# Bias of an FFN sublayer added by a one-row fp32 matmul instead of on VectorE

## The chip, the cores and the metric

The kernel runs on all 8 cores of one Trainium2 chip. Each core takes one batch element (2048 x 1024, fp32) and works alone; the weights are the same for all. The metric is device time in microseconds (us) of the slowest core. Lower is better.

## The reference, cut to what matters

```python
x = x + 0.5 * ffn(layernorm(x), w, bias)
x = x + attn(layernorm(x), Wq, Wk, Wv, W_G, W_O)     # retention, 8 heads, silu gate
x = x + 0.5 * ffn(layernorm(x), w, bias)

def ffn(x, weight, bias):
    # both operands: blocks of 32 along the last axis, scale = max|block| / 7.5,
    # each value / scale rounded to the nearest value of a 6-bit float grid
    xd = quantize(x) * scale_x
    wd = quantize(weight) * scale_w
    return xd @ wd.T + bias
```

The change is about the last line of `ffn`, its bias, and the `x + 0.5 * ...` around it. Both FFN sublayers use the same weight and bias.

## The kernel before, in words

The kernel is written engine by engine, with the order of each engine's work and all semaphore waits set by hand. `emit` is called once for each engine; `c.op(engine, ...)` issues only on that engine and `c.wait(engine, sem, value)` blocks it. Work is in order on each engine. The core's 2048 rows are 16 row chunks `rc` of 128 rows by 1024 columns, and `x_sb` holds all 16 in SBUF.

The program goes: load of x and constants; LayerNorm statistics on ScalarE; quantization and transposition of the FFN weight (first sublayer only, eight chunks); the first FFN's loop over 16 row chunks; the attention sublayer (statistics, transposes, four projections, heads, output projection); LayerNorm statistics; the second FFN's loop; the store.

The loop of `ffn_sublayer`, for row chunk `rc` in program order:

- `q_stageA(rc)` on VectorE: block maxima (TENSOR_REDUCE), scales, reciprocal, scaled values.
- `q_yy(rc)` on ScalarE: squares of these. `x_B2(rc-1)` on VectorE: the end of the previous chunk's rounding, which waits for the previous chunk's cast.
- `ffn_evac(rc-2)` on VectorE: takes the product of chunk `rc-2` out of PSUM. Two instructions: a SCALAR_TENSOR_TENSOR that makes `ffntmp = 0.5 * psum + bias_half`, then a TENSOR_TENSOR `x_sb += ffntmp`. It waits for the matmuls of that chunk (`mm_done[rc-2]`).
- `q_B1(rc)` on VectorE (six instructions), `q_cast(rc)` on ScalarE behind it.
- `x_d(rc+2)` on ScalarE: the activation that centres the rows of a later chunk. Chunks 16 and up do not exist, so the last two rounds have none.
- `x_tr(rc-1)`: eight 128 x 128 transposes on TensorE, each copied out of PSUM by ScalarE, two PSUM tiles in turn. By their semaphore counts the transposes start behind `q_cast(rc)` and `x_d(rc+2)`.
- `x_mm(rc-1)` on TensorE: 16 bf16 matmuls of 128 x 512 into one half of `psc` (two halves of 512 columns, eight contraction chunks each).

So the matmuls that `ffn_evac(rc-2)` waits for were put in motion by the cast at the end of `q_B1(rc-1)`, one round earlier. Behind the loop come `x_B2(15)`, `ffn_evac(14)`, `x_tr(15)`, `x_mm(15)` and `ffn_evac(15)`.

`bias_half` is the bias vector in all 128 partitions. At the start it is multiplied by 0.5 in place on VectorE, behind the wait for the first loads.

In the profile all instructions stand at line 60, that of the helper `op`; they are told apart by engine, operation, tile and shape. `arena` is the SBUF memory, `psc` the PSUM area of the large products, `pt` the two transpose tiles.

Of the kernel before, what the change touches and what calls it, by code (L numbers as in the profile page):

```python
# [12 lines left out]
ALU = mybir.AluOpType  # L13
# [7 lines left out]
KC = 8  # L21
# [62 lines left out]
def build_program(stop_after="full"):  # L84
# [23 lines left out]
    O_C = 196608  # L108
# [12 lines left out]
    def vf32(off, n):  # L121
        return A[:, off:off + 4 * n].bitcast(F32)

    def vbf(off, n):
        return A[:, off:off + 2 * n].bitcast(BF16)
# [4 lines left out]
    x_sb = vf32(O_X, RC * D).rearrange("p (rc d) -> p rc d", d=D)  # L130
# [5 lines left out]
    xdt_sb = vbf(O_V, KC * S).rearrange("p (k n) -> p k n", n=S)  # L136
    g_sb = vbf(O_G, RC * D).rearrange("p (rc d) -> p rc d", d=D)
    wbf_sb = vbf(O_W, KC * D).rearrange("p (k d) -> p k d", d=D)
    wdt_sb = wbf_sb
# [8 lines left out]
    ffntmp = vf32(O_S + 4096, D)  # L148
# [14 lines left out]
    bias_half = vf32(O_C, D)  # L163
# [14 lines left out]
    yv_sb = [vf32(O_C + 9344, 128), vf32(O_C + 9856, 128)]  # L178
    zrow_sb = [vbf(O_C + 10368, 128), vbf(O_C + 10624, 128)]
    negm_sb = vf32(O_C + 10880, 16)  # L180

    sem_ctx = ExitStack()
    sems = {k: sem_ctx.enter_context(nc.semaphore(k)) for k in SEMS}

    def emit(c: Ctx):
# [3 lines left out]
        for i in range(4):  # L189
# [3 lines left out]
             in_=bias_dr.partition_broadcast(128)).inc("ld", 16)  # L193
        c.op("sync", "dma_start", out=m128_sb, in_=m128_dr).inc("ld", 16)
        c.op("sync", "dma_start", out=id_sb, in_=id_dr).inc("ld", 16)
        c.wait("vector", "ld")
        c.op("vector", "tensor_scalar", bias_half, bias_half, 0.5, None,
             ALU.mult).inc("v")
        c.fence()

        def ln_stats(src3d, eps):
# [119 lines left out]
        def ffn_sublayer(build_wdt):  # L321
# [90 lines left out]
            def x_mm(k, s_after):  # L412
                fp = psc[:, (k % 2) * 1024:(k % 2) * 1024 + 1024]
                c.wait("tensor", "s", s_after)
                if k >= 2:
                    c.wait("tensor", "v", ev_done[k - 2])
                for jh in range(2):
                    for kc in range(KC):
                        ins = c.op("tensor", "matmul",
                                   fp[:, jh * 512:(jh + 1) * 512],  # L420
                                   xdt_sb[:, kc, k * 128:(k + 1) * 128],
                                   wdt_sb[:, kc, jh * 512:(jh + 1) * 512],
                                   start=(kc == 0), stop=(kc == KC - 1),
                                   skip_group_check=True)
                        if jh == 1 and kc == KC - 1:
                            ins.inc("t")
                mm_done[k] = c.cnt["t"]

            def ffn_evac(rc):
                fp = psc[:, (rc % 2) * 1024:(rc % 2) * 1024 + 1024]  # L430
                c.wait("vector", "t", mm_done[rc])
                c.wait("vector", "v")
                c.op("vector", "scalar_tensor_tensor", ffntmp, fp, 0.5,
                     bias_half, ALU.mult, ALU.add).inc("v")
                ev_done[rc] = c.cnt["v"]
                c.wait("vector", "v")
                c.op("vector", "tensor_tensor", x_sb[:, rc, :],
                     x_sb[:, rc, :], ffntmp, ALU.add).inc("v")

            x_d(0, max(negm_v, w_end_v))  # L440
            x_d(1, max(negm_v, w_end_v))
            for rc in range(RC):
                if _PARANOID:
                    c.fence()
                c.wait("vector", "s", sd[rc])
                xy[rc] = q_stageA(rc % 2, db[rc % 2], ln_rstd[:, rc:rc + 1])
                xyy[rc] = q_yy(rc % 2, xy[rc])
                if rc >= 1:
                    x_B2(rc - 1)
                if rc >= 2:  # L450
                    ffn_evac(rc - 2)
                xtq[rc] = q_B1(rc % 2, xyy[rc])
                xcast[rc] = q_cast(rc % 2, xtq[rc])
                if rc + 2 < RC:
                    x_d(rc + 2, xxd[rc - 1] if rc >= 1 else xy[rc])
                if rc >= 1:
                    s_after = x_tr(rc - 1)
                    x_mm(rc - 1, s_after)
            x_B2(RC - 1)
            ffn_evac(RC - 2)  # L460
            s_after = x_tr(RC - 1)
            x_mm(RC - 1, s_after)
            ffn_evac(RC - 1)

        ffn_sublayer(build_wdt=True)
# [153 lines left out]
        for hc in range(_NHEADS):  # L619
            for nh in range(2):  # L620
# [20 lines left out]
                for mc in range(MMAX):  # L641
# [10 lines left out]
                    for nb in range(nblo, 2 * nh + 2):  # L652
                        slot = psc[:, (pp % 4) * 512:(pp % 4) * 512 + 512]
                        if piece_rel[pp % 4] is not None:
# [5 lines left out]
                             start=True, stop=True).inc("t")  # L660
# [108 lines left out]
        for rc in range(RC):  # L769
# [10 lines left out]
            for jh in range(2):  # L780
                for kc in range(H):
                    ins = c.op("tensor", "matmul",
                               wp[:, jh * 512:(jh + 1) * 512],
                               zt_sb[:, kc, rc * 128:(rc + 1) * 128],
                               wbf_sb[:, kc, jh * 512:(jh + 1) * 512],
                               start=(kc == 0), stop=(kc == H - 1),
                               skip_group_check=True)
# [23 lines left out]
    with nc.Block() as block:  # L811
        @block.sync
        def _(e):
            emit(Ctx(nc, "sync", sems))

        @block.vector
        def _(e):
            emit(Ctx(nc, "vector", sems))

        @block.scalar  # L820
        def _(e):
            emit(Ctx(nc, "scalar", sems))

        @block.tensor
        def _(e):
            emit(Ctx(nc, "tensor", sems))

        @block.gpsimd
        def _(e):
            emit(Ctx(nc, "gpsimd", sems))  # L830
# [38 lines left out]
```

How the kernel before makes its waits and increments, by code:

```python
    def inc(self, sem, n=1):  # L42
        self.ctx.cnt[sem] += n
        if self.inst is not None:
            self.inst.then_inc(self.ctx.sems[sem], n)
        return self
# [16 lines left out]
    def wait(self, eng, sem, val=None):  # L63
        v = self.cnt[sem] if val is None else val
        if v <= 0:
            return
        if self.cur == eng:
            getattr(self.nc, eng).wait_ge(self.sems[sem], v)
```

## Time and profile before

| | us |
|---|---|
| median of 3 runs | 1866.97 (1866.2 to 1868.91) |
| the profiled execution | 1866.82 |
| its span, slowest core (core 2) | 1865.2 |
| spans of the 8 cores | 1858.7 to 1865.2 |
| VectorE busy | 1053.2 (56%) |
| TensorE matmul busy | 762.2 (41%) |
| ScalarE busy | 535.8 (29%) |

The span is from the first to the last instruction on the core; the execution's own time is 1.6 us more. Busy shares are means over stages that have different limits. The first FFN's loop lies between about 232 and 557 us, the second one's between about 1515 and 1836 us. The granted TensorE clock (PEclk) is a share of 2.4 GHz: 1.00 is 2.4 GHz and 0.50 is 1.2 GHz.

### The profile page before, as it was taken

The numbers are of one execution on the slowest core, as the hardware profiler recorded it, in microseconds if no ns is written. First come the engines' busy times: TensorE is split into PE (matmuls) and PEld (weight loads), VectorE is DVE, ScalarE is ACT, GpSimd is POOL, SyncE is SP. The second block draws the span as 40 slices with busy tenths as digits, with TensorE's granted clock in tenths as the row PEclk, the third lists the DMA queues.
The fourth block names the chain that finished last, engine by engine and source line by source line (L and its number), as shares of the span: only waits on it lengthen the run. The fifth ranks groups of instructions, "written<-read, shape, count | busy, mean of one in ns | idle before, by whom it ended". The sixth has DMA issues, their size and how long they took to land.

```text
span 1865.2 us, 15347 instructions; the slowest of 8 cores (1858.7 to 1865.2 us)
## 1 busy us (share of the span) xinstructions
PE 762.2 (41%) x3776; PEld 352.1 (19%) x3776; DVE 1053.2 (56%) x1525; ACT 535.8 (29%) x1414; POOL 20.8 (1%) x41
## 2 busy tenths in 40 slices
PE   0001123234340556849685445555419213334332
PEld 0000001111110222324242233333204001111110
DVE  0399799999970233320115555555533179999982
ACT  2612222222228500003234444444410632222220
POOL 0000000000000100000000000000001000000000
PEclk9999987666765578879896777776759656555566
DMA  7000100000000464540200000000034200000005
GB/s 215 23 23 23 46 0 0 1 0 1 0 1 27 169 181 139 161 154 4 68 1 1 1 1 1 1 1 1 1 113 125 78 0 1 0 1 1 0 0 181
DMA packets 18853, 81.27 MB, mean 44 GB/s; under 512 B 2000, under 2 KB 2000, under 8 KB 16464
## 3 DMA queue, kind: packets, MB, share of 16 engines
q1 hardware_dynamic: 11904, 53.02, 9.1%
q0 software_dynamic: 6864, 27.27, 4.2%
q8 instruction: 35, 0.57, 0.1%
q14 instruction: 50, 0.41, 0.1%
HBM read 61.41 MB, written 18.87 MB: 43 GB/s over the span
## 4 chain that ended last, share of the span: by engine, by line
DVE 39%; PE 28%; ACT 12%; issue 11%; DMA 6%; DVEq 1%; SPq 1%; ACTq 0%; POOL 0%; POOLq 0%
DVE arena L60 39%; PE psc L60 21%; ACT arena L60 12%; PE pbig L60 4%; PE pt L60 2%; DMA arena<-wo 1%; DVEq L68 1%; DMA arena<-wk 1%; DMA arena<-wv 1%; DMA arena<-wq 1%; DMA arena<-ident 1%; SPq L60 1%; DMA arena<-wg 1%; ACTq L68 0%; POOL out L60 0%
## 5 line engine op out<-in xcount | busy, mean ns | idle before, releaser
L60 PE MATMUL psc<-arena 128*128 128x512 bf16 x2112 | 580.1, 430 | 138.3 <-DVE arena L60 118.6
L60 PE MATMUL pt<-arena 128*128 128x128 bf16 x576 | 133.7, 263 | 929.1 <-ACT arena L60 508.2
L60 DVE TENSOR_SCALAR arena<-arena 128x1024 f32<-128x1024 f32 (+4 forms) x348 | 169.9, 508 | 272.5 <-ACT arena L60 188.1
L60 DVE TENSOR_TENSOR arena<-arena 128x1024 f32<-128x1024 f32 (+3 forms) x347 | 285.7, 823 | 37.6 <-DVE arena L60 1.8
L60 PEld LDWEIGHTS psc<-arena 128*128 128x128 bf16 x2112 | 219.9, 107 | 426.0 <-issue 261.2
L60 DVE SCALAR_TENSOR_TENSOR arena<-arena 128x1024 f32<-128x1024 int32 (+3 forms) x211 | 240.4, 1139 | 29.5 <-ACT arena L60 7.9
L60 PEld LDWEIGHTS pt<-arena 128*128 128x128 bf16 x576 | 60.2, 104 | 1011.4 <-issue 999.9
L60 ACT ACTIVATE arena<-arena 128x1024 f32<-128x1024 f32 (+2 forms) x187 | 184.2, 986 | 151.3 <-DVE arena L60 142.8
L60 ACT CAST arena<-arena 128x1024 int32<-128x1024 f32 x40 | 41.8, 1044 | 534.1 <-DVE arena L60 534.1
L60 ACT CAST arena<-psc 128x512 bf16<-128x512 f32 (+1 forms) x224 | 106.0, 495 | 293.2 <-DMA arena<-wg 189.6
L60 ACT COPY arena<-pt 128x128 bf16<-128x128 bf16 x576 | 134.6, 265 | 179.9 <-PE pt L60 178.9
L60 DVE TENSOR_TENSOR arena<-psc,arena 128x128 bf16<-128x128 f32 (+1 forms) x192 | 81.4, 424 | 175.3 <-PE psc L60 164.3
L60 DVE CAST arena<-arena 128x1024 bf16<-128x1024 f32 x40 | 27.7, 694 | 150.1 <-PE psc L60 58.3
L60 PE MATMUL pbig<-arena 128*128 128x128 bf16 x1088 | 98.8, 229 | 2.6
L60 PEld LDWEIGHTS pbig<-arena 128*128 128x128 bf16 x1088 | 78.6, 103 | 42.3 <-issue 20.4
L60 DVE CAST arena<-psc 128x512 bf16<-128x512 f32 x96 | 66.4, 692 | 27.6 <-PE psc L60 26.5
L60 DVE TENSOR_SCALAR arena<-pbig,arena 128x128 f32<-128x128 f32 x128 | 52.2, 408 | 16.9 <-ACT arena L60 16.7
L60 DVE TENSOR_REDUCE arena<-arena 128x32 f32<-128x1024 f32 x40 | 48.5, 1213 | 5.8 <-ACT arena L60 5.8
L60 ACT ACTIVATE arena<-pbig 128x128 f32<-128x128 f32 x128 | 35.5, 277 | 43.8 <-DVE arena L60 33.5
L60 DVE SCALAR_TENSOR_TENSOR arena<-psc,arena 128x1024 f32<-128x1024 f32 x32 | 39.2, 1225 | 12.8 <-PE psc L60 8.2
L60 DVE TENSOR_TENSOR arena<-arena,psc 128x1024 f32<-128x1024 f32 x16 | 19.5, 1221 | 40.0 <-PE psc L60 40.0
L60 ACT ACTIVATE arena<-psc 128x512 bf16<-128x512 f32 x32 | 19.1, 597 | 33.9 <-PE psc L60 33.9
(13 smaller groups left out, 105.4 us busy)
## 6 DMA issues: line engine op xcount, KB each, us to landing
arena<-x SPq DMA_DIRECT2D x4, 2048.0 KB, 19.3
xspill<-arena POOLq DMA_DIRECT2D x16, 512.0 KB, 3.1
arena<-qsc SPq DMA_DIRECT2D x8, 1024.0 KB, 5.5
arena<-ksc SPq DMA_DIRECT2D x8, 1024.0 KB, 5.7
arena<-xspill POOLq DMA_DIRECT2D x16, 512.0 KB, 4.2
out<-arena POOLq DMA_DIRECT2D x4, 2048.0 KB, 15.9
arena<-wf SPq DMA_DIRECT2D x8, 512.0 KB, 3.2
arena<-wq SPq DMA_DIRECT2D x8, 512.0 KB, 4.2
```

What stands on the lines that cost most here:

```text
L60: inst = getattr(getattr(self.nc, eng), name)(*a, **k)
L68: getattr(self.nc, eng).wait_ge(self.sems[sem], v)
```

## The change

The bias is taken into the product by one more matmul for each half of 512 columns, and VectorE's second instruction for each chunk goes away:

```diff
+    ones_row = vf32(O_C + 10944, 128)[0:1, :]
...
+        c.op("vector", "memset", ones_row, 1.0).inc("v")
         c.wait("vector", "ld")
-        c.op("vector", "tensor_scalar", bias_half, bias_half, 0.5, None,
-             ALU.mult).inc("v")
...
                 for jh in range(2):
                     for kc in range(KC):
-                        ins = c.op("tensor", "matmul",
+                        c.op("tensor", "matmul",
...
-                                   start=(kc == 0), stop=(kc == KC - 1),
-                                   skip_group_check=True)
-                        if jh == 1 and kc == KC - 1:
-                            ins.inc("t")
+                             start=(kc == 0), stop=False,
+                             skip_group_check=True)
+                    ins = c.op("tensor", "matmul", fp[:, jh * 512:(jh + 1) * 512],
+                               ones_row,
+                               bias_half[0:1, jh * 512:(jh + 1) * 512],
+                               start=False, stop=True, skip_group_check=True)
+                    if jh == 1:
+                        ins.inc("t")
...
-                c.op("vector", "scalar_tensor_tensor", ffntmp, fp, 0.5,
-                     bias_half, ALU.mult, ALU.add).inc("v")
+                c.op("vector", "scalar_tensor_tensor", x_sb[:, rc, :], fp,
+                     0.5, x_sb[:, rc, :], ALU.mult, ALU.add).inc("v")
                 ev_done[rc] = c.cnt["v"]
-                c.wait("vector", "v")
-                c.op("vector", "tensor_tensor", x_sb[:, rc, :],
-                     x_sb[:, rc, :], ffntmp, ALU.add).inc("v")
```

The added matmul contracts over one partition: its stationary operand is a row of 128 ones, its moving operand 512 columns of the bias, both fp32, while the other matmuls are bf16. The 0.5 of `bias_half` is now applied with that of the product, in the one instruction that remains.

VectorE around `ffn_evac` in the first FFN's loop, before (the rows from the end of `x_B2` to the first of the next `q_stageA`):

```order
L60 TENSOR_TENSOR arena<-arena 128x1024 [waits v] x3
L60 SCALAR_TENSOR_TENSOR arena<-psc,arena 128x1024 [waits t,v]
L60 TENSOR_TENSOR arena<-arena 128x1024 [waits v]
L60 TENSOR_SCALAR arena<-arena 128x1024 [waits s]
L60 TENSOR_SCALAR arena<-arena 128x1024
L60 SCALAR_TENSOR_TENSOR arena<-arena 128x1024 [waits v]
L60 TENSOR_SCALAR arena<-arena 128x1024 [waits v]
L60 SCALAR_TENSOR_TENSOR arena<-arena 128x1024 [waits v]
L60 TENSOR_TENSOR arena<-arena 128x1024 [waits v]
L60 TENSOR_REDUCE arena<-arena 128x32 [waits s]
```

And the same place now:

```order
L60 TENSOR_TENSOR arena<-arena 128x1024 [waits v] x3
L60 SCALAR_TENSOR_TENSOR arena<-psc,arena 128x1024 [waits t,v]
L60 TENSOR_SCALAR arena<-arena 128x1024 [waits s]
L60 TENSOR_SCALAR arena<-arena 128x1024
L60 SCALAR_TENSOR_TENSOR arena<-arena 128x1024 [waits v]
L60 TENSOR_SCALAR arena<-arena 128x1024 [waits v]
L60 SCALAR_TENSOR_TENSOR arena<-arena 128x1024 [waits v]
L60 TENSOR_TENSOR arena<-arena 128x1024 [waits v]
L60 TENSOR_REDUCE arena<-arena 128x32 [waits s]
```

The instruction that reads `psc` still waits for TensorE (`t`); the one behind it is gone, and `q_B1` follows at once.

TensorE in the same loop, before and then now, as the difference prints it (`pt` are the transposes of a chunk, `psc` its product):

```order
-L60 MATMUL psc<-arena 128x512 x16
-L60 MATMUL pt<-arena 128x128 x8
-L60 MATMUL psc<-arena 128x512 x16
+L60 MATMUL psc<-arena 128x512 x18
+L60 MATMUL pt<-arena 128x128 x8
+L60 MATMUL psc<-arena 128x512 x18
```

Each product has 18 instructions for 16: the ninth and the eighteenth are the added fp32 ones, and the eighteenth is the one that releases `ffn_evac`.

## Rows read from the trace of the kernel before

**Rows 1.** The page, part 1: busy us of each engine, share, instructions.

```profile
PE 762.2 (41%) x3776; PEld 352.1 (19%) x3776; DVE 1053.2 (56%) x1525; ACT 535.8 (29%) x1414; POOL 20.8 (1%) x41
```

**Rows 2.** Stretches: from:to, length, busy of PE, PEld, DVE, ACT, POOL; PEclk, DMA.

```profile
232.00:557.30 325.30, 112.12 (x384) 43.02 (x384) 291.08 (x311) 73.76 (x173) 0.00 (x0) 0.70 0.00 0
1515.00:1836.00 321.00, 119.21 (x384) 44.68 (x384) 287.19 (x305) 71.41 (x171) 0.00 (x0) 0.60 0.00 0
```

**Rows 3.** Timeline, one round, first FFN: start us, length, engine, line, operation [idle before].

```profile
361.25 0.15 PEld L60 LDWEIGHTS psc<-arena 128*128 128x128 bf16 x1 [0.28 <-issue]
...
361.68 0.15 PEld L60 LDWEIGHTS psc<-arena 128*128 128x128 bf16 x1 [0.28 <-issue]
...
365.50 1.23 DVE L60 SCALAR_TENSOR_TENSOR arena<-psc,arena 128x1024 f32<-128x1024 f32 x1
366.83 1.23 DVE L60 TENSOR_TENSOR arena<-arena 128x1024 f32<-128x1024 f32 x1
367.97 1.29 DVE L60 TENSOR_SCALAR arena<-arena 128x1024 f32<-128x1024 f32 x2
...
373.96 1.21 DVE L60 TENSOR_REDUCE arena<-arena 128x32 f32<-128x1024 f32 x1
374.14 1.04 ACT L60 CAST arena<-arena 128x1024 int32<-128x1024 f32 x1 [14.27 <-DVE arena L60]
...
379.03 0.27 ACT L60 COPY arena<-pt 128x128 bf16<-128x128 bf16 x1 [0.33 <-PE pt L60]
...
379.55 5.20 PE L60 MATMUL psc<-arena 128*128 128x512 bf16 x16 [0.61 <-ACT arena L60]
...
385.89 1.23 DVE L60 SCALAR_TENSOR_TENSOR arena<-psc,arena 128x1024 f32<-128x1024 f32 x1
```

**Rows 4.** Timeline of TensorE, both FFN loops: products of one chunk each.

```profile
256.81 5.13 PE L60 MATMUL psc<-arena 128*128 128x512 bf16 x16 [0.50 <-ACT arena L60]
...
318.37 5.07 PE L60 MATMUL psc<-arena 128*128 128x512 bf16 x16 [0.61 <-ACT arena L60]
...
481.52 5.41 PE L60 MATMUL psc<-arena 128*128 128x512 bf16 x16 [0.61 <-ACT arena L60]
...
542.00 5.89 PE L60 MATMUL psc<-arena 128*128 128x512 bf16 x16 [0.61 <-ACT arena L60]
550.88 3.61 PE L60 MATMUL psc<-arena 128*128 128x512 bf16 x16 [0.61 <-ACT arena L60]
...
1535.37 5.84 PE L60 MATMUL psc<-arena 128*128 128x512 bf16 x16 [0.50 <-ACT arena L60]
...
1780.59 6.11 PE L60 MATMUL psc<-arena 128*128 128x512 bf16 x16 [0.61 <-ACT arena L60]
```

**Rows 5.** Stretches in and behind one product; the third number from the right is PEclk.

```profile
359.20:362.00 2.80, 2.80 (x7) 0.95 (x8) 2.59 (x4) 0.67 (x1) 0.00 (x0) 0.50 0.00 0
362.60:364.30 1.70, 1.70 (x8) 0.58 (x6) 1.49 (x3) 0.00 (x0) 0.00 (x0) 1.00 0.00 0
364.40:370.00 5.60, 0.00 (x0) 0.00 (x0) 5.29 (x6) 0.00 (x0) 0.00 (x0) 0.92 0.00 0
```

**Rows 6.** Timeline of VectorE: first and last evacuation of each loop, and the last addition.

```profile
263.19 1.23 DVE L60 SCALAR_TENSOR_TENSOR arena<-psc,arena 128x1024 f32<-128x1024 f32 x1
...
554.66 1.23 DVE L60 SCALAR_TENSOR_TENSOR arena<-psc,arena 128x1024 f32<-128x1024 f32 x1 [4.04 <-PE psc L60]
555.99 1.23 DVE L60 TENSOR_TENSOR arena<-arena 128x1024 f32<-128x1024 f32 x1
...
1541.75 1.23 DVE L60 SCALAR_TENSOR_TENSOR arena<-psc,arena 128x1024 f32<-128x1024 f32 x1
...
1832.40 1.23 DVE L60 SCALAR_TENSOR_TENSOR arena<-psc,arena 128x1024 f32<-128x1024 f32 x1 [4.16 <-PE psc L60]
1834.08 1.22 DVE L60 TENSOR_TENSOR arena<-arena 128x1024 f32<-128x1024 f32 x1 [0.46 <-DVE arena L60]
```

**Rows 7.** Timeline of the program's start: the multiplication of the bias.

```profile
32.45 0.69 DVE L60 TENSOR_SCALAR arena<-arena 128x1024 f32<-128x1024 f32 x1 [32.45 <-DMA arena<-ident]
```

More of the change, by code:

```diff
@@ L418, in x_mm @@
                     for kc in range(KC):
-                        ins = c.op("tensor", "matmul",
-                                   fp[:, jh * 512:(jh + 1) * 512],
-                                   xdt_sb[:, kc, k * 128:(k + 1) * 128],
-                                   wdt_sb[:, kc, jh * 512:(jh + 1) * 512],
-                                   start=(kc == 0), stop=(kc == KC - 1),
-                                   skip_group_check=True)
-                        if jh == 1 and kc == KC - 1:
-                            ins.inc("t")
+                        c.op("tensor", "matmul",
+                             fp[:, jh * 512:(jh + 1) * 512],
+                             xdt_sb[:, kc, k * 128:(k + 1) * 128],
+                             wdt_sb[:, kc, jh * 512:(jh + 1) * 512],
+                             start=(kc == 0), stop=False,
[6 more added lines that the diff above has]
+                        ins.inc("t")
                 mm_done[k] = c.cnt["t"]
```

## The prediction

> **What bounds the kernel now.** I read the busy times first: VectorE leads with 1053.2 us of 1865.2, TensorE has 762.2 [rows 1]. That is a mean over stages, so I went on to the stretches. In the two FFN loops VectorE is busy 291.1 of 325.3 us and 287.2 of 321.0, TensorE only 112.1 and 119.2 [rows 2]. By that view anything taken off VectorE is gained and anything put on TensorE is hidden. The timeline of one round says how far this holds. The reader should follow two paths from one moment, the end of `q_B1` (where TENSOR_REDUCE starts, 373.96) [rows 3]:
>
> - VectorE's path: `q_stageA`, `x_B2`, then it is ready to evacuate at 385.89, which is 11.93 us later.
> - The other path: cast at 374.14, then the centring activation, eight transposes with their copies (the last copy starts at 379.03), the product at 379.55, which takes 5.20 us and ends at 384.75. That is 10.79 us after the same moment.
>
> So the product that the evacuation waits for is ready only 1.14 us before VectorE asks for it. Where VectorE does wait for a product, at the loop's end, it starts 0.17 us behind the product's end (550.88 + 3.61 = 554.49, then 554.66) [rows 4, 6], which leaves about 0.97 us of cover. A round takes 20.39 us (365.50 to 385.89) [rows 3].
>
> **What goes.** The second instruction of `ffn_evac`: 366.83 - 365.50 = 1.33 us of VectorE's order [rows 3], since the next instruction, at 367.97, then follows the evacuation at the distance of 1.14 at which it follows the addition now. If VectorE kept the bound, a round would be 20.39 - 1.33 = 19.06 us. The doubling of the evacuated tile's role (x_sb as input and output) is costed at nothing: operands, shape and type are those of the 1.23 us row.
>
> At the start the bias multiplication goes, 0.69 us, and about 0.08 of its hand-over: -0.77 us, on the path, since all engines wait behind it [rows 7]. The memset of one partition lies under the 32 us of loading.
>
> **What comes.** Two matmuls of 128 x 512 with fp32 operands for each chunk, behind the 8th and the 16th bf16 one, 64 in all. Call the time of a pair F. No fp32 matmul is in this trace, so I bound it by the bf16 rows of the same shape. At the high clock 16 of them take 3.61 us, 0.226 each [rows 4]; at the low clock one follows another at 361.68 - 361.25 = 0.43 us [rows 3]. Low end: an fp32 one costs as much as a bf16 one at the high clock, F = 0.45. High end: fp32 operands are split into two halves each, so that four partial products stand for one, all at the low clock: F = 8 x 0.43 = 3.44. I take four products for each matmul at the high clock, 8 x 0.226 = 1.81, plus one exposed weight load each at the 0.15 us of a load beside a product [rows 3], an estimate for loads that the split operand may need in between: F = 2.11. I go by the high-clock row because the clock is 0.50 early in a product, 1.00 at its end, and still 0.92 on average in the 5.6 us behind it [rows 5]: matmuls that are hung on the end meet the high clock. "FP8 and Floating Point Precision" of the Trainium skill, TensorE Precision Notes, says that true fp32 goes four times through the array; no row here shows it, and by it alone F would be 1.81.
>
> F is larger than the cover of 0.97, so the product becomes what ends last, and the evacuation waits. Behind it in VectorE's order stands `q_B1`, whose cast starts the next transposes and product, so the wait is handed on in full. The round is then a chain: from the end of `q_B1` to the product 5.59 (379.55 - 373.96); the product; 0.17; the evacuation 1.14; `q_B1` 5.99 (373.96 - 367.97) [rows 3].
>
> **The clock's part in the product.** A product at the high clock throughout takes 3.61 us. Each us by which the clock's rise comes later after its start costs 1 - 0.226 / 0.43 = 0.47 us. With x for that lateness, a product is 3.61 + 0.47x now and 3.61 + F + 0.47x after. The rows give x = 3.2 for the first product (5.13), 3.8 at 481.52 (5.41), 4.7 at 1535.37 (5.84), and 5.3 at most (6.11, at 1780.59) [rows 4]. Between 318.37 and 481.52 lie 8 rounds of 20.39 us, in which the product grew from 5.07 to 5.41: 0.0425 a round, so x grew by 0.09. The rises thus came 20.48 us apart, while the products came 20.39 apart. This matters for the sum: a round of the new chain is
>
> 5.59 + 3.61 + F + 0.47x + 0.17 + 1.14 + 5.99 = 16.50 + F + 0.47x.
>
> If it is shorter than 20.48, x grows from round to round and lengthens it; if longer, x shrinks. It settles at 20.48 as long as the x needed lies within what the clock does, about 2.4 (a gap to the largest seen, my choice) to 5.3. With F = 2.11: 18.61 + 0.47x = 20.48 at x = 4.0. So I expect the 1.33 us taken from VectorE to return as a wait for TensorE, and the round to be 20.48 for 20.39.
>
> **The sum**, F = 2.11, evacuations numbered 0 to 15.
>
> First FFN. Evacuation 0: 256.81 + 5.13 + 2.11 + 0.17 = 264.22, against 263.19 [rows 4, 6]. Twelve rounds: 12 x 20.48, less 0.8 while x goes from 3.2 to 4.0 (a deficit of 0.47 of the distance, which shrinks by 0.53 each round, sums to the distance): 245.0. Round 13 has no centring activation in front of its transposes, about 1.06 us, of which 0.5 returns as later clock: 19.9. Round 14: 1.14 + 5.99 + 4.53 + product + 0.17, product 3.61 + 2.11 + 0.47x with x at 5.3 (8.2) or, if the clock rises earlier, near 2.8 (7.0): about 19.5. Last: 550.88 - (542.00 + 5.89) = 2.99 for the transposes [rows 4], 3.61 and F: 8.7. Sum 293.1, so evacuation 15 is at 557.3 and the loop ends at 558.6 (one instruction of 1.23 behind it), against 555.99 + 1.23 = 557.2 [rows 6]: +1.4.
>
> Second FFN. Evacuation 0: 1535.37 + 5.84 + 2.28 = 1543.5. Rounds: 245.8 + 0.7 (x comes down from 4.7), 19.9, 19.5, 8.7: 294.6. End 1838.1 + 1.2 = 1839.4, against 1835.3 [rows 6]: +4.1.
>
> Start: -0.8. Total +4.7 us on the profiled execution's 1866.82, which is 1871.5; the median shown is 0.15 above that execution: 1871.7. What a measurement of this kernel can tell from no change is about 0.2%, 3.7 us. In this regime a us of F is worth about 8 us in all (1 at the first evacuation, 2 in the rounds and 1 at the last product, twice): F = 1.81 gives 1869, F = 2.9 gives 1878.
>
> **Rivals.**
>
> A. The fp32 matmul is cheap and VectorE keeps the bound. For it: one partition is contracted, and at one bf16 price (F = 0.45) a round has 16.95 + 0.47x, under 19.06 up to x = 4.5. Against it: the operands have twice the width. Price: 26 rounds x -1.33 = -34.6, ends -2, start -0.8: about 1830. At twice the bf16 price, F = 0.90, the x needed to settle would be 6.6, out of reach; a round averages 17.4 + 0.47 x 4 = 19.3: 26 x -1.1 = -29, ends and start -2: 1836. "Perfetto Trace Analysis" of the Trainium skill, Engine Utilization, counts an fp32 low/high mode at half the output rate, which would be that second case; no run here shows it yet. Below F = 1.4 (x above 5.3) this rival decides. Chance 0.18.
>
> B. Slower, by the clock and the weight loads. The added matmuls use one of 128 rows and stand in the middle and at the end of a product; if the clock falls or rises late over them, or if each of the partial products exposes its weight load, F goes to 3.44. Then 16.50 + 3.44 needs x = 1.2, which is out of reach; a round averages 19.94 + 0.47 x 4 = 21.8: 26 x 1.4 = +37, ends +4: 1907. With no rise at all a product would be 16 x 0.43 + 3.44 = 10.3 and a round 23.2, +73: 1942. For it: the low clock already covers half of each product. Against it: the 0.92 behind a product [rows 5]. It decides from F = 2.9 on (x below 2.4). Chance 0.22.
>
> C. The edit is neutral within the settled regime: F between 1.4 and 2.0, -1 to +3.7 us. It is the lower part of my own case, which as a whole has 0.60; I give this part 0.22.
>
> **How the numbers follow.** Settled rounds 0.60, with 1866 to 1878 as their own range; A 0.18; B 0.22. Faster by over 0.2%: A and a little for rounds that do not settle but stay near the 19.8 of x = 3, 0.21. Within 0.2%: 0.23. Slower: the rest, 0.56. The range reaches to B's first case and leaves out most of A: 1857 to 1905.
>
> **What would show it.** In the profile after: fp32 matmuls of some 0.9 to 1.05 us each in the high clock (right), under 0.5 (A), 1.7 (B). The evacuation from `psc` preceded by about 1.4 us of idle time released by PE in nearly every round (right), none (A). Products of 7.5 to 8 us with a steady length and rounds of 20.48 us, drawn towards it within some four rounds from below in the first FFN. VectorE busy less by 32 x 1.23 = 39 us and the total still not below 1866. I am wrong if rounds are at 19.06 to 19.5, or if the clock in the added matmuls is 0.50.

## The result, and the profile after

| | before | after |
|---|---|---|
| median, us | 1867.41 (8 runs) | 1893.9 (8 runs, 1890.8 to 1906.6) |
| profiled execution / span | 1866.82 / 1865.2 | 1894.76 / 1893.2 |
| spans of the 8 cores | 1858.7 to 1865.2 | 1877.7 to 1893.2 |

The ratio is 1.0133, 95% interval 1.0094 to 1.0172: the change makes the kernel 1.3% slower. Ratios here and below are formed from undisturbed executions alone, so a median can lie off its ratio. The time is inside the stated range (1857 to 1905), on the side forecast, but 22 us above the 1871.7 of the likeliest case.

The page's part 1 and its line of the chain that ended last, after (compare [rows 1]):

```profile
PE 858.7 (45%) x3904; PEld 371.2 (20%) x3904; DVE 1013.0 (54%) x1493; ACT 540.6 (29%) x1414; POOL 20.8 (1%) x41
PE 42%; DVE 23%; ACT 14%; issue 12%; DMA 6%; SPq 1%; DVEq 1%; ACTq 0%; POOL 0%; POOLq 0%
```

VectorE lost 40 us of work and the kernel lost none of its time. In the chain VectorE had 39% and TensorE 28% before; now it is 23% and 42%. The groups by shape (busy us, mean ns, idle time in front and what ended it) show what took VectorE's place:

```profile
L60 DVE SCALAR_TENSOR_TENSOR arena<-psc,arena 128x1024 f32<-128x1024 f32 x32 | 39.2, 1225 | 88.4 <-PE psc L60 74.7 <-PE pt L60 13.7
...
L60 PE MATMUL psc<-arena 1*128 1x512 f32 x128 | 85.7, 753 | 0.0
...
L60 PEld LDWEIGHTS psc<-arena 1*128 1x128 f32 x128 | 22.8, 222 | 42.5 <-issue 42.5
```

The 32 evacuations now wait 88.4 us, where the page of before has 12.8, 8.2 of it at the two ends. The 64 added matmuls appear as 128 records: each is two instructions with a weight load of its own.

**A settled round.** Timeline of core 5, first FFN (compare [rows 3]):

```profile
442.16 1.22 DVE L60 SCALAR_TENSOR_TENSOR arena<-psc,arena 128x1024 f32<-128x1024 f32 x1 [1.55 <-PE psc L60]
449.30 1.21 DVE L60 TENSOR_REDUCE arena<-arena 128x32 f32<-128x1024 f32 x1
...
454.88 7.60 PE L60 MATMUL psc<-arena 128*128 128x512 bf16 x20 [0.61 <-ACT arena L60]
...
462.65 1.23 DVE L60 SCALAR_TENSOR_TENSOR arena<-psc,arena 128x1024 f32<-128x1024 f32 x1 [1.54 <-PE psc L60]
```

The product starts 5.58 us behind TENSOR_REDUCE, takes 7.60 us, and the evacuation follows 0.17 us later after 1.54 us of idling. The round is 20.49 us. This is the round that was forecast, to 0.01 us.

The same regime was there before the change, on cores that the prediction did not look at. On core 1 of the kernel before, in the first loop:

```profile
420.11 6.25 PE L60 MATMUL psc<-arena 128*128 128x512 bf16 x16 [0.61 <-ACT arena L60]
...
426.53 1.22 DVE L60 SCALAR_TENSOR_TENSOR arena<-psc,arena 128x1024 f32<-128x1024 f32 x1 [0.19 <-PE psc L60]
```

The product is longer than core 2's 5.20 us, since the clock rises later in it (an inference from the length). The evacuation waits for it and starts 0.17 us behind its end, and five rounds in a row there are 20.47 or 20.48 us. So the cover of 1.14 us is that of core 2. On this core it was used up already, in that loop.

**Rounds in which the clock does not rise.** The same core's products at the start of the first loop and at the end of the second (compare [rows 4]):

```profile
256.05 11.10 PE L60 MATMUL psc<-arena 128*128 128x512 bf16 x20 [0.50 <-ACT arena L60]
...
303.92 11.10 PE L60 MATMUL psc<-arena 128*128 128x512 bf16 x20 [0.61 <-DVE arena L60]
327.91 11.10 PE L60 MATMUL psc<-arena 128*128 128x512 bf16 x20 [0.61 <-ACT arena L60]
351.90 7.88 PE L60 MATMUL psc<-arena 128*128 128x512 bf16 x20 [0.61 <-ACT arena L60]
...
1816.13 11.10 PE L60 MATMUL psc<-arena 128*128 128x512 bf16 x20 [0.61 <-ACT arena L60]
1839.35 9.90 PE L60 MATMUL psc<-arena 128*128 128x512 bf16 x20 [0.61 <-ACT arena L60]
1852.39 10.16 PE L60 MATMUL psc<-arena 128*128 128x512 bf16 x20 [0.61 <-ACT arena L60]
```

The first four of the first loop (two of them shown) take 11.10 us each, 3.5 us more than a settled one. TensorE works for 11 us without a pause and its clock stays at 1.2 GHz. In the stretches (third number from the right) this reads, for the product at 1816.13 and for the settled one at 434.38:

```profile
1816.20:1819.50 3.30, 3.30 (x8) 0.91 (x8) 3.02 (x4) 0.64 (x1) 0.00 (x0) 0.50 0.00 0
1821.80:1827.10 5.30, 5.30 (x10) 1.40 (x8) 1.51 (x2) 0.00 (x0) 0.00 (x0) 0.50 0.00 0
434.40:437.50 3.10, 3.10 (x8) 0.96 (x8) 2.89 (x4) 0.68 (x1) 0.00 (x0) 0.50 0.00 0
438.50:440.10 1.60, 1.60 (x7) 0.51 (x6) 1.50 (x2) 0.00 (x0) 0.00 (x0) 1.00 0.00 0
```

The price of an added matmul at either level can be read from the weight loads around it:

```profile
571.40 0.29 PEld L60 LDWEIGHTS psc<-arena 1*128 1x128 f32 x2 [0.73 <-issue]
...
574.29 0.29 PEld L60 LDWEIGHTS psc<-arena 1*128 1x128 f32 x2 [0.42 <-issue]
...
1819.63 0.50 PEld L60 LDWEIGHTS psc<-arena 1*128 1x128 f32 x2 [0.84 <-issue]
...
1825.15 0.50 PEld L60 LDWEIGHTS psc<-arena 1*128 1x128 f32 x2 [0.84 <-issue]
```

From one fp32 load to the next lie one fp32 matmul and eight bf16 ones. High clock: 574.29 - 571.40 = 2.89, less 8 x 0.226, is 1.08 us; low clock: 5.52, less 8 x 0.43, is 2.08. A pair (F) is 2.16 or 4.2 us.

**All rounds** of core 5, as distances between the starts of its evacuations in us, 15 in each loop:

```
first FFN   23.89 23.99 23.99 20.77 20.63 20.55 20.52 20.50 20.49 20.49 20.48 20.48 | 21.59 19.40 10.49
second FFN  20.27 20.57 20.39 20.39 20.43 20.46 20.46 20.67 20.39 20.43 20.45 20.47 | 23.28 22.03 13.30
```

The settling at 20.48, from above or below, is in both; it is on all eight cores. The excess over the forecast stands at the two ends: at the start on some cores, in the last three distances on all of them. Of the 44 products of 9 us and more on the eight cores, 32 stand at the same four places on every core (one near the end of the first loop, the last three of the second).

### The profile page after: what moved, and what is told of

It reads as the page before. It is cut to its first block, busy times and chain, and to the rows that moved or that the text cites. A ratio compares the mean times of both kernels' runs of the same rounds, so it can differ in the third digit from the quotient of the medians.

```text
span 1893.2 us, 15539 instructions; the slowest of 8 cores (1877.7 to 1893.2 us)
## 1 busy us (share of the span) xinstructions
PE 858.7 (45%) x3904; PEld 371.2 (20%) x3904; DVE 1013.0 (54%) x1493; ACT 540.6 (29%) x1414; POOL 20.8 (1%) x41
## 4 chain that ended last, share of the span: by engine, by line
PE 42%; DVE 23%; ACT 14%; issue 12%; DMA 6%; SPq 1%; DVEq 1%; ACTq 0%; POOL 0%; POOLq 0%
PE psc L60 34%; DVE arena L60 23%; ACT arena L60 14%; PE pbig L60 4%; PE pt L60 4%; DMA arena<-wo 1%; DMA arena<-wk 1%; DMA arena<-wq 1%; DMA arena<-wv 1%; DMA arena<-ident 1%; SPq L60 1%; DVEq L68 1%; DMA arena<-wg 1%; ACTq L68 0%; DMA arena<-xspill 0%
## 5 line engine op out<-in xcount | busy, mean ns | idle before, releaser
L60 PE MATMUL psc<-arena 128*128 128x512 bf16 (+1 forms) x2240 | 672.4, 452 | 134.6 <-DVE arena L60 115.5
L60 PE MATMUL pt<-arena 128*128 128x128 bf16 x576 | 138.1, 263 | 866.6 <-ACT arena L60 474.8
L60 PEld LDWEIGHTS psc<-arena 128*128 128x128 bf16 (+1 forms) x2240 | 239.4, 113 | 480.3 <-issue 317.2
L60 DVE TENSOR_TENSOR arena<-arena 128x1024 f32<-128x1024 f32 (+4 forms) x315 | 246.5, 782 | 34.3 <-DVE arena L60 1.8
L60 ACT COPY arena<-pt 128x128 bf16<-128x128 bf16 x576 | 139.4, 265 | 182.4 <-PE pt L60 181.4
L60 DVE SCALAR_TENSOR_TENSOR arena<-psc,arena 128x1024 f32<-128x1024 f32 x32 | 39.2, 1225 | 88.4 <-PE psc L60 74.7
```

The source lines that it names most:

```text
L60: inst = getattr(getattr(self.nc, eng), name)(*a, **k)
```

## The experiments

In the profile of each kernel I count products of 9 us and more, of 256 (two loops, 16 chunks, 8 cores), from the start and end of their matmuls. The kernel before has none (longest 6.5 us), the changed one 44. The count says something for the long versions alone: with one bf16 matmul added to each half, a product at 1.2 GHz from end to end would be about 8 us (an estimate from matmuls 0.43 us apart).

Two theories were open on these. Theory 1: the added matmuls contract over a single row, and such work does not bring TensorE's clock up as other matmuls do. Theory 2: it is fp32, or the mere length, that shifts the product against the clock.

| added matmul | place | rows | median, us | ratio to before (95%) | products >= 9 us | longest |
|---|---|---|---|---|---|---|
| fp32 (the change) | behind | 1 | 1893.9 | 1.0133 (1.0094 to 1.0172) | 44 | 11.1 |
| fp32 | behind | 64 | 1883.2 | 1.0076 (1.0046 to 1.0105) | 19 | 10.2 |
| fp32 | behind | 128 | 1872.3 | 1.0026 (1.0014 to 1.0038) | 0 | 8.2 |
| 4 x bf16 | behind | 1 | 1883.1 | 1.006 (1.0039 to 1.0082) | 31 | 10.7 |
| 4 x bf16 | behind | 128 | 1870.8 | 1.0006 (0.9976 to 1.0037) | 0 | 8.2 |
| 1 x bf16 | behind | 1 | 1839.5 | 0.985 (0.9834 to 0.9866) | 0 | 7.2 |
| 1 x bf16 | behind | 128 | 1834.0 | 0.9801 (0.9738 to 0.9864) | 0 | 6.9 |
| fp32 | ahead | 1 | 1837.0 | 0.9834 (0.9817 to 0.9852) | 0 | 8.4 |
| 1 x bf16 | ahead | 128 | 1829.0 | 0.9786 (0.9747 to 0.9825) | 0 | 7.0 |
| none, bias left out | - | - | 1827.9 | 0.9767 (0.9704 to 0.983) | 0 | 6.5 |
| fp32, old evacuation kept | behind | 1 | 1971.3 | 1.0542 (1.0486 to 1.0599) | 171 | 11.1 |

### fp32, 128 rows deep

```diff
-    ones_row = vf32(O_C + 10944, 128)[0:1, :]
+    ones_row = vf32(O_C + 10944, 128)
-        c.op("vector", "memset", ones_row, 1.0).inc("v")
+        c.op("vector", "memset", ones_row, 1.0 / 128).inc("v")
-                               bias_half[0:1, jh * 512:(jh + 1) * 512],
+                               bias_half[:, jh * 512:(jh + 1) * 512],
```

> The added fp32 matmul at the same place and of the same length, but 128 rows deep: 128 x 128 weights of 1/128 and the bias in all 128 partitions. Theory 1 (one-row matmuls are what keeps the clock from rising): no product of over 9 us in the loops, rounds settle at 20.48, the last three distances between evacuations sum to about 48 us in both FFNs (51.5 and 58.6 in the changed kernel), total 1870 to 1877. Theory 2 (fp32, with its doubled weight loads and gaps, is what keeps it low): products of 9.7 to 11.1 us at the same places as in the changed kernel, total 1885 to 1900.

Measured 1872.3. The last three products of its second loop, at the places where the changed kernel has 11.10, 9.90 and 10.16:

```profile
1805.97 7.93 PE L60 MATMUL psc<-arena 128*128 128x512 bf16 x20 [0.61 <-ACT arena L60]
1826.02 8.14 PE L60 MATMUL psc<-arena 128*128 128x512 bf16 x20 [0.61 <-ACT arena L60]
1837.15 5.33 PE L60 MATMUL psc<-arena 128*128 128x512 bf16 x20 [0.61 <-ACT arena L60]
```

Rounds settle at 20.48; the last three distances sum to 48.4 and 48.7 us (core 5), and 22 us are gone, as theory 1 has it. But the depth is not all that changed. The last product runs at the high clock throughout and takes 5.33 us, where 16 bf16 matmuls take 3.61 [rows 4]: its pair takes 1.72 us, and not the 2.16 us of the one-row pair, although the expectation calls them equally long. By the prediction's 8 us for each us of F that is worth about 3.5 of the 22 us. The version with 64 rows, below, holds the length.

### Four bf16 matmuls, one row deep

```diff
-                    ins = c.op("tensor", "matmul", fp[:, jh * 512:(jh + 1) * 512],
-                               ones_row,
-                               bias_half[0:1, jh * 512:(jh + 1) * 512],
-                               start=False, stop=True, skip_group_check=True)
+                    for i4 in range(4):
+                        ins = c.op("tensor", "matmul",
+                                   fp[:, jh * 512:(jh + 1) * 512], ones_row,
+                                   bias_bf[0:1, jh * 512:(jh + 1) * 512],
+                                   start=False, stop=(i4 == 3), ...)
```

`bias_bf` is the bias cast to bf16 (here a quarter of it) behind the first fence, when VectorE is idle.

> For each fp32 one-row matmul, four bf16 one-row matmuls of a quarter of the bias: nearly the same length (F = 1.81 at the high clock), one row deep, no fp32. Theory 1 (one row keeps the clock low): products of 9 us and more appear as in the changed kernel, above all in the last rounds, total 1878 to 1893. Theory 2 (fp32 keeps it low): no such products, rounds settle at 20.48, total 1867 to 1873.

Measured 1883.1, with 31 slow products. Without fp32 they are still there. The third last product of its second loop (core 4), and the loads of the added matmuls in its last one:

```profile
1815.23 9.75 PE L60 MATMUL psc<-arena 128*128 128x512 bf16 x24 [0.61 <-ACT arena L60]
...
1851.12 0.54 PEld L60 LDWEIGHTS psc<-arena 1*128 1x128 bf16 x4 [0.84 <-issue]
...
1853.92 0.54 PEld L60 LDWEIGHTS psc<-arena 1*128 1x128 bf16 x4 [0.42 <-issue]
```

Here 1853.92 - 1851.12 = 2.80, less 8 x 0.226, is 0.99 us for four one-row bf16 matmuls at the high clock, about 2.0 for the pair, and not the 1.81 of the expectation.

### Four bf16 matmuls, 128 rows deep

The same with `ones_row` and `bias_bf` over all partitions and weights of 1/128.

> As the kernel with four bf16 one-row matmuls in place of each fp32 one, but 128 rows deep (weights 1/128, a quarter of the bias in all partitions). It is the fourth corner of the two by two. Theory 1 (only the depth of one row keeps the clock from rising): same as the fp32 one of 128 rows less the exposed weight loads: no product over 9 us, rounds settle at 20.48, total 1866 to 1872. Theory 2 (any lengthening by some 2 us gives the slow products of the last rounds): 9.7 us products in round 13 as with one row, total 1875 to 1885.

Measured 1870.8, no slow product. In this two by two the slow products occur one row deep and not 128 rows deep, in both types; the type changes how many there are (44 or 31). But the length goes along with the depth: this version's last product takes 5.34 us, so its pair takes 1.73 us as with fp32, against 2.16 and 2.0 us one row deep. The four corners alone do not part depth from length.

### fp32, 64 rows deep

```diff
+    ones_row = vf32(O_C + 10944, 128)[0:64, :]
+        c.op("vector", "memset", ones_row, 1.0 / 64).inc("v")
+                               bias_half[0:64, jh * 512:(jh + 1) * 512],
```

> The added fp32 matmul at its place in the changed kernel, 64 rows deep (weights 1/64). If what the clock answers to grows with the rows in use, 64 rows lie between: no or few products over 9 us, total 1871 to 1880, nearer to the 1872 of 128 rows than to the 1894 of one. If only a full array counts, it is as with one row: 1885 to 1895.

Measured 1883.2, halfway, and 3 us above the range of the first reading, so the expectation is half a miss: 64 rows lie between one and 128, and not near 128.

This version is the cleanest test of depth, since its pair is as long as the one-row pair: settled products take 7.59 us in both, with the clock rising at the same place. Two neighbouring products of the first loop on core 5, in the changed kernel and then with 64 rows:

```profile
516.34 7.59 PE L60 MATMUL psc<-arena 128*128 128x512 bf16 x20 [0.61 <-DVE arena L60]
535.77 9.75 PE L60 MATMUL psc<-arena 128*128 128x512 bf16 x20 [0.61 <-ACT arena L60]
...
503.03 7.59 PE L60 MATMUL psc<-arena 128*128 128x512 bf16 x20 [0.61 <-DVE arena L60]
522.46 8.11 PE L60 MATMUL psc<-arena 128*128 128x512 bf16 x20 [0.61 <-ACT arena L60]
```

The first product is the same and the second starts 19.43 us behind it in both. Then the one-row version takes 9.75 us and the one with 64 rows 8.11; the other seven cores show the same. Type, length, place and distance are equal here, so depth is what is left: theory 1 holds, and theory 2 does not explain this product. From 64 to 128 rows the pair also gets shorter and the clock rises elsewhere in the product, so how much of those 11 us is depth is not shown.

Sixteen of the 19 slow products are the last two of the first loop, on each of the eight cores: distance 13 is 19.95 as with 128 rows, distances 14 and 15 are 21.85 and 13.36 against 18.52 and 9.95.

### One bf16 matmul, one row deep

```diff
-                               bias_half[0:1, jh * 512:(jh + 1) * 512],
+                               bias_bf[0:1, jh * 512:(jh + 1) * 512],
```

> The added matmul stays one row deep and behind each half's product, but in bf16 (bias row cast to bf16 once, behind the first fence, while VectorE idles). Chain theory (the product's length sets the round): a pair costs 0.45 us in place of 2.16, a round of the chain is 16.95 + 0.47x, below VectorE's own 19.06 up to x = 4.5, so rounds of 19.06 to 19.5, idle time before the evacuation near nothing, total 1830 to 1840. Rival (in a one-row matmul the clock does not count the array as busy, whatever its length, and that alone makes the slow rounds): products of 9 us and more still show up and the total stays above 1860.

Measured 1839.5, at the upper end. Rounds still go from 19.06 to 20.43. The pair is longer than the 0.45 us assumed. A product at the high clock throughout (core 5):

```profile
1798.18 4.35 PE L60 MATMUL psc<-arena 128*128 128x512 bf16 x18 [0.61 <-ACT arena L60]
```

4.35 - 3.61 = 0.74 us: between matmuls of 128 rows, a one-row matmul costs more than one of 128 rows.

### One bf16 matmul, 128 rows deep, behind

The same with `ones_row` and `bias_bf` over all partitions and weights of 1/128.

> As the bf16 one-row version (1839), at the same place behind each half, but 128 rows deep. Theory 1: the rounds of 19.3 to 20.4 of that version came from late clock rises caused by the one-row matmuls; they go, rounds are 19.06, and the total is 1829 to 1834. Theory 2: those rounds come from the chain's length alone (F = 0.45 with the clock drifting through its positions); nothing changes, 1838 to 1841.

Measured 1834.0, just at the first range's edge. Rounds over 20 us are gone but for single ones, rounds of 19.6 to 19.8 stay. So both theories have a part in this case: depth is worth 5 us, and a chain of 16.95 + 0.47x does exceed 19.06 where x passes 4.5. The 5 us hold both effects of depth, the shorter pair (4.04 us for a product at the high clock throughout, so 0.43 for 0.74) and the clock. No run parts them.

### fp32, one row, ahead of the transposes

```diff
+            def x_bias(k):
+                fp = psc[:, (k % 2) * 1024:(k % 2) * 1024 + 1024]
+                if k >= 2:
+                    c.wait("tensor", "v", ev_done[k - 2])
+                for jh in range(2):
+                    c.op("tensor", "matmul", fp[:, jh * 512:(jh + 1) * 512],
+                         ones_row, bias_half[0:1, jh * 512:(jh + 1) * 512],
+                         start=True, stop=False, skip_group_check=True)
+
             def x_tr(k):
+                x_bias(k)
```

The product then continues the accumulation (`start=False`).

> The same fp32 one-row matmuls, but issued first in each chunk's accumulation, ahead of the chunk's transposes, where TensorE stands idle for some 9 us a round. Nothing else is changed. Chain theory: F leaves the chain, a round is the larger of VectorE's 19.06 and 16.5 + 0.47x, so 19.06 to 19.4; total 1829 to 1838. Rival (what costs is the disturbance of the clock by one-row matmuls, wherever they are): rounds stay at or above 20.4 and the total near 1867 or above.

Measured 1837.0. The same 64 matmuls that make the change 66 us slower than the version with no bias at all cost 9 us when they stand in TensorE's idle time, behind one product's release and ahead of the next transposes. Most rounds are 19.06. The larger part of those 9 us is at the ends: the last distance is 10.1 to 11.0 us, 6.6 to 8.2 with no bias, since at the end the last chunk's pair stands between a product and transposes that could follow at once.

### The bias left out

> The bias is left out altogether: no added matmul (F = 0), the evacuation keeps its single instruction. It prices the removal alone. Chain theory: the chain is 16.5 + 0.47x, under VectorE's 19.06 for every x up to 5.4, so all rounds at 19.06 (a few at 19.4), 26 rounds x 1.33 = 35 us, 3 us at the two ends, 0.8 at the start: 1826 to 1831. Rival (a shorter round shifts the clock's rise so that part of the gain is lost even without any added matmul): rounds of 19.3 and more on average, total 1835 or more.

Measured 1827.9: the removal alone is worth 39 us, the sum's 26 x 1.33 + 3 + 0.8 = 38.

### bf16, 128 rows, ahead

The matmuls stand as in the version ahead with fp32, with the 128-row bf16 operands described above.

> The version that the runs so far point to: the bias by bf16 matmuls of 128 rows, first in the accumulation, issued ahead of the transposes where TensorE is idle. F is off the chain, short, and counted by the clock as any other matmul. Chain theory: rounds of 19.06, last product as in the kernel before, total 1827 to 1833. Rival (an added burst ahead of the transposes shifts the clock's rise whatever its kind): same as the fp32 one-row version ahead, 1837, with last distances of 10 to 11 us.

The first series gave only two times that can be used, 1831.5 and 1828.1, and was repeated:

> A repeat of the version with bf16 matmuls of 128 rows ahead of the transposes, for an interval, since its first series had only two undisturbed times (1831.5 and 1828.1). Chain theory: 1827 to 1833, a ratio of 0.979 to 0.982. Rival (its two good times were lucky in the clock's position): 1834 to 1840.

Measured 1829.0, ratio 0.9786. Two neighbouring rounds of it, with no idle time in front of the evacuation:

```profile
409.38 5.62 PE L60 MATMUL psc<-arena 128*128 128x512 bf16 x18 [0.61 <-ACT arena L60]
...
415.72 1.23 DVE L60 SCALAR_TENSOR_TENSOR arena<-psc,arena 128x1024 f32<-128x1024 f32 x1
...
428.43 6.32 PE L60 MATMUL psc<-arena 128*128 128x512 bf16 x18 [0.61 <-ACT arena L60]
...
434.77 1.23 DVE L60 SCALAR_TENSOR_TENSOR arena<-psc,arena 128x1024 f32<-128x1024 f32 x1
```

Each row is 16 matmuls of one product and, right behind them, the two of the next chunk's bias, which nobody waits for yet. (So the lengths in the table take in the next chunk's pair in the two versions ahead.) It differs from the version that leaves the bias out by 1.1 us, which the two intervals cannot tell from nothing. This kernel beats both the one before and the changed one, by 2.1% and 3.4% (1829.0 against 1893.9). The bias is rounded to bf16 in it.

### The matmuls added, the old evacuation kept

> One half of the change alone: the fp32 one-row matmuls are added (with a row of zeros, so that they add nothing), VectorE keeps both instructions and the bias multiplication. Chain theory: the chain grows by the 1.33 us that the changed kernel took out, a round is 16.5 + 2.16 + 1.33 + 0.47x = 19.99 + 0.47x; it would need x = 1.0 to settle at 20.48, which the clock did not do in any run, so rounds do not settle: 21.1 and more, with more products of 9 to 11 us than in the changed kernel; total 1915 to 1960. Rival (the clock's pace sets the round at 20.48 whatever VectorE does, and the removal was worth nothing): total 1890 to 1900, as the changed kernel.

Measured 1971.3, above the range given. The mechanism is the expected one and the price was set too low. Rounds do not settle: on core 3 they go 25.3, 21.6, 24.4, 24.1, 24.0, 25.3, 21.6, ... over and over, and 171 products take 9 us or more. So the halves of the change do not add up: the matmuls alone cost 105 us, the removal alone brings 39, and together they cost 26.

## Why the prediction was right or wrong

- **Cover.** On the core that the prediction read, the product was ready 1.14 us before its evacuation [rows 3], and an F of 2.16 used that up and more. Shown by the evacuation's idle time and by the two versions with F off the chain or short (1837.0, 1839.5).
- **F.** Taken as 2.11, measured 2.16 at the high clock, four times a bf16 matmul's time and some 0.17 us more for each. The 0.17 us belongs to the one-row weights: with 128 rows a pair took 1.72. The four passes of the Trainium skill, "FP8 and Floating Point Precision", TensorE Precision Notes, agree with that 1.72 us: 0.86 for an fp32 matmul is 3.8 times the 0.226 of a bf16 one. The half rate in "Perfetto Trace Analysis" of the Trainium skill, Engine Utilization, does not hold for the whole matmul, as the second case of rival A took it (F = 0.90); it would fit each of the two instructions that the trace shows for one fp32 matmul, 0.43 us apiece. With F above 1.4 rival A fell.
- **The settled round** of 20.48 us was right in all four long versions placed behind the product (one or 128 rows, fp32 or four bf16), and in the one of 64 rows, with pairs of 1.72 to 2.16 us; the 1.33 us taken from VectorE came back as a wait.
- **The sum** gave 1871.7. The version with 128 rows took 1872.3, but with its F of 1.72 the sum would be about 1868.6, so that the agreement to 0.6 us is in part luck. What does agree are the loops: 294.3 and 294.5 us from first to last evacuation on its slowest core, forecast 293.1 and 294.6. The stretch between the loops took 989.2 us there, forecast 986.2; it differs by up to 8 us from core to core in the kernel before (979.3 to 987.1). I had priced the matmul as one that the clock treats like its neighbours.
- **What failed** is one step, the reason for pricing F at the high clock ("matmuls that are hung on the end meet the high clock"), and with it the bound of 5.3 put on x in the last rounds. With one row the rise came later or not at all; the prediction's own sign of being wrong, a clock of 0.50 in the added matmuls, appeared in part of the rounds. The bound was also read on one core: on other cores of the kernel before products reach 6.5 us, which is x = 6.1. On core 5 the first three distances are 71.9 for 3 x 20.48 = 61.4, +10.4. The last three of the first loop are 51.5 for the 48.1 forecast, +3.4, and of the second 58.6 for 48.1, +10.5. These 24 us are about the miss of 22. The profiled core is another one than before (5 for 2). Its first evacuation comes at 267.3 for the 264.2 forecast, and the stretch between its loops takes 983.2 us for 986.2: +3.1 and -3.0, which cancel.
- **Rival B** named this ("the added matmuls use one of 128 rows") and gave 1907 to 1942 for it at every round. It holds in part of the rounds, 44 products of 256, and is thus an addition to the settled case and not its opposite. I had treated the two as exclusive, which is why the likeliest value was too low. That the range held is partly luck: its upper part was put there for B's dearer F at every round, not for a few rounds without a rise.
- **Same or slower.** The 0.56 on slower was right for the change, but of the 26 us by which it is slower the forecast mechanism gives about 5; the rest comes from the step that failed. In the 128-row version the ratio is 1.0026, at the edge of what can be told.

## What to carry to other kernels

Before work is moved off the busiest engine, follow the next latest path into each of its waits: here the product was ready 1.1 us before the busy engine asked for it on one core, and not a moment before on another, and the moved work lengthened that product by 2.2. Read the margin on more than one core. Put such work where the receiving engine is idle (in front of the transposes, as the start of the accumulation) instead of behind its longest burst. And make a helper matmul as deep and as narrow in type as its neighbours, if its operand may be rounded: bf16, 128 rows, and in the idle time was 65 us faster than fp32, one row, and behind, for the same sum but for the bias's rounding.

## What the runs showed of the hardware

- A stream of matmuls can keep TensorE busy for 11.1 us without its clock leaving 1.2 GHz, when two stretches of about 2 us in it are one row deep. With 128 rows in the same places, where the two stretches are also shorter, this did not happen in any of 256 products; with 64 rows 19 took 9 us or more. At equal length and distance, one row against 64 made a product 9.75 us for 8.11, on all eight cores.
- An fp32 matmul of 128x512 shows as two instructions. At 2.4 GHz it took 0.86 us with 128 rows, where neighbours are bf16 with 128 rows, and 1.08 with one row; at 1.2 GHz 2.08 with one row.
- A matmul of one row between matmuls of 128 rows cost more than one of 128 rows: in bf16 0.74 us a pair against 0.43 at 2.4 GHz.
- In this case the loop that is bound by a product whose clock rises on the way settles to a fixed round: 20.48 us in five kernels whose added pairs differ in type, depth and time (1.72 to 2.16 us), and on some cores of the kernel before, with no added pair. Inside this regime a pair longer by 0.44 us (64 rows against 128) left the round as it was.
- In the stretches PEclk reads 1.00 where no change of the clock has been recorded yet, as in the product at 303.92 of the changed kernel, whose weight loads are 0.43 us apart and whose length is that of the low clock:

```profile
303.90:308.00 4.10, 4.08 (x9) 1.50 (x10) 3.78 (x5) 0.73 (x1) 0.00 (x0) 1.00 0.00 0
```
